# A decoder layer: folded cross-attention weights stored as two arrays, high and low, instead of one

## What is computed

```python
x = x + self_attention(layernorm(x), weight_qkv, weight_proj)   # 32 heads, 8 key/value groups, head size 128
x = x + cross_attention(layernorm(x), ctx, ctx, Wq, bq, Wk, bk, Wv, bv, interference, amp, Wo, bo)
x = x + ffn(layernorm(x), ...)                                  # low-rank weights multiplied out, one matmul

# in the cross attention, per projection:
y = z @ W.T + bias                       # reshaped to heads x 16 x 4
y = y + 0.1 * amp * einsum('bhsdi,hij->bhsdj', y, interference)
```

## Time and profile before

| | |
|---|---|
| median of three runs | 3618.52 us (3617.93 to 3620.3) |
| profiled execution, its own time | 3618.95 us |
| its span, first to last instruction | 3616.8 us |
| mean granted TensorE clock | 0.977 of full speed |
| busy in the span: PE / PE weight loads | 3440.5 us (95%) / 2677.0 us |
| busy: DVE / POOL / ACT | 1494.1 / 1250.3 / 1185.0 us |
| moved by DMA | 431.16 MB, mean 119 GB/s |
| self phase / cross phase / FFN (about) | 0 to 2036 / 2036 to 3268 / to 3617 us |

### The profile page before, as it was taken

The page is one execution under the profiler, slowest core; times in us unless marked ns, Lnnn a source line. Parts: engine busy times, 40 slices in busy tenths (PEclk is TensorE's granted clock), DMA queues, the critical chain, the costliest instruction groups (busy, mean ns, idle before and its releaser), DMA issues. The chain is left out here.

```text
span 3616.8 us, 49438 instructions
## 1 busy us (share of the span) xinstructions
PE 3440.5 (95%) x18100; PEld 2677.0 (74%) x18100; DVE 1494.1 (41%) x2238; ACT 1185.0 (33%) x1679; POOL 1250.3 (35%) x563
## 2 busy tenths in 40 slices
PE   6999999999999999999999679989979999998999
PEld 5888887888878888878787467767767777763587
DVE  3232332323332232423232446656656665652453
ACT  3232232323233232323222235445444454440110
POOL 4334343434324343434342334434334443320000
PEclk9999999999999999999999889999999999999999
DMA  4323233323333232332221254544555455534032
GB/s 168 106 94 113 89 135 130 115 93 106 127 128 117 93 110 93 128 134 89 85 93 53 108 150 128 173 146 137 156 152 137 129 161 162 141 88 157 35 133 76
DMA packets 137253, 431.16 MB, mean 119 GB/s; under 512 B 24112, under 2 KB 24112, under 8 KB 137144
## 3 DMA queue, kind: packets, MB, share of 16 engines
q1 hardware_dynamic: 131384, 408.58, 35.1%
q10 hardware_dynamic: 5760, 20.97, 1.4%
HBM read 316.21 MB, written 37.75 MB: 98 GB/s over the span
## 5 line engine op out<-in xcount | busy, mean ns | idle before, releaser
L446 POOL TENSOR_TENSOR sa_wl<-sa_wraw,sa_wh 128x1024 fp32r<-128x1024 f32 x192 | 458.2, 2402 | 777.3 <-ACT sa_wh L597 777.3
L53 PE MATMUL sa_u<-sa_ln_xh,sa_wh 128*128 128x512 f32 x1536 | 628.5, 409 | 4.4 <-DVE sa_ln_xl L254 4.4
L54 PE MATMUL sa_u<-sa_ln_xl,sa_wh 128*128 128x512 f32 x1536 | 599.7, 390 | 0.0
L55 PE MATMUL sa_u<-sa_ln_xh,sa_wl 128*128 128x512 f32 x1536 | 599.3, 390 | 0.0
L457 POOL TENSOR_TENSOR sa_pl<-sa_praw,sa_ph 128x1024 fp32r<-128x1024 f32 x128 | 318.0, 2516 | 446.4 <-ACT sa_ph L649 446.4
L53 PE MATMUL sa_pr<-sa_ph,sa_oh 128*128 128x512 f32 x1024 | 428.6, 419 | 0.1
L746 DVE TENSOR_TENSOR sa_acc<-sa_pr,sa_acc 128x512 f32<-128x512 f32 x256 | 176.9, 692 | 569.3 <-PE sa_pr L55 569.3
L54 PE MATMUL sa_pr<-sa_pl,sa_oh 128*128 128x512 f32 x1024 | 400.8, 391 | 0.0
L55 PE MATMUL sa_pr<-sa_ph,sa_ol 128*128 128x512 f32 x1024 | 400.0, 391 | 0.0
L738 DVE TENSOR_TENSOR sa_ol<-sa_o,sa_oh 128x512 fp32r<-128x512 f32 x128 | 88.6, 692 | 718.5 <-ACT sa_oh L661 718.5
L53 PEld LDWEIGHTS sa_u<-sa_ln_xh,sa_wh 128*128 128x128 f32 x1536 | 289.3, 188 | 83.6 <-issue 24.2
(11 more groups left out here) (185 smaller groups left out, 5765.7 us busy)
## 6 DMA issues: line engine op xcount, KB each, us to landing
sa_wraw<-in_wqkv SPq DMA_DIRECT2D x192, 512.0 KB, 3.5
sa_praw<-in_wproj SPq DMA_DIRECT2D x128, 512.0 KB, 3.5
ca_wraw<-w_folded SPq DMA_DIRECT2D x96, 512.0 KB, 3.2
ca_kstack<-ca_kmh SPq DMA_DIRECT2D x256, 128.0 KB, 2.4
ca_wraw<-in_wo SPq DMA_DIRECT2D x33, 512.0 KB, 4.2
ca_kstack<-ca_kml SPq DMA_DIRECT2D x128, 128.0 KB, 2.4
ca_qstack<-ca_qh SPq DMA_DIRECT2D x256, 64.0 KB, 2.5
sa_nat<-in_w_nat SPq DMA_DIRECT2D x24, 512.0 KB, 4.7
```

The lines of the kernel that those rows point to most:

```text
L53: nc.tensor.matmul(out, ah, bh, start=(first and i == 0), stop=False)
L54: nc.tensor.matmul(out, ah, bl, start=False, stop=False)
L55: ins = nc.tensor.matmul(out, al, bh, start=False, stop=(last and i == len(parts) - 1))
L446: nc.gpsimd.tensor_tensor(wl[:, u % 3], wraw[:, u % 3], f32(wh[:, u % 3]), ALU.subtract).then_inc(w_split, 1)
```

## The change

1. Self phase: ACT's copy of each fold half is now made to an fp32r tile `foldh`; DVE gets a new step `low_fold`, which subtracts it from the bank into `foldl`, and now DVE, not ACT, frees `v_ps` (`v_copied`). ACT waits for it before `store_fold`, which issues two stores of 512 KB instead of one.
2. Cross phase: SP loads high and low parts straight into `wh` and `wl` (two loads of 512 KB per chunk). ACT's copies and POOL's subtractions of key, query and value weights are gone. `wo` still comes raw and is split.
3. SP's order: a chunk's loads for the next step wait until PE has used the old one (`u_done`), no longer for a free raw buffer. The key's stand between the key stacks and the `wo` load, the query's behind the query stacks, the value's at the end of the step, ahead of a cross step's stores. The accumulator loads of the first step stand behind no weights of the next step.

```diff
@@ self_attention_phase: scalar
-            act.sem_inc(fold_stored, 16)
+            act.sem_inc(fold_stored, 32)
...
                     act.wait_ge(folded, m * 2 + (half + 3))
                     if half == 0:
-                        act.wait_ge(fold_stored, m * 16 + 16)
-                    nc.scalar.activation(fold[:, half * HALF:(half + 1) * HALF], v_ps[:], ACT.Copy
-                                         ).then_inc(v_copied, 1)
+                        act.wait_ge(fold_stored, m * 32 + 32)
+                    nc.scalar.activation(foldh[:, half * HALF:(half + 1) * HALF], v_ps[:], ACT.Copy
+                                         ).then_inc(fold_hi, 1)
...
                     act.wait_ge(v_copied, v0 + 4)
-                    act.dma_start(tile_of(w_folded, m), fold[:]).then_inc(fold_stored, 16)
+                    act.dma_start(tile_of(w_folded_hi, m), f32(foldh[:])).then_inc(fold_stored, 16)
+                    act.dma_start(tile_of(w_folded_lo, m), f32(foldl[:])).then_inc(fold_stored, 16)
@@ self_attention_phase: vector
+                def low_fold(half):
+                    if not s.steady:
+                        return
+                    dve.wait_ge(fold_hi, m * 2 + (half + 1))
+                    cols = slice(half * HALF, (half + 1) * HALF)
+                    nc.vector.tensor_tensor(foldl[:, cols], v_ps[:], f32(foldh[:, cols]), ALU.subtract
+                                            ).then_inc(v_copied, 1)
...
                 low_o(0)
                 next_moments(0)
+                low_fold(0)
                 low_o(1)
                 next_moments(1)
                 add_projected(0)
+                low_fold(1)
@@ cross_attention_phase: sync
-            def weights(n, item, g, skipped=0):
-
-                if not (isinstance(n, int) and n < 0):
-                    sp.wait_ge(w_split, splits(n, item + (-2), skipped))
...
+            def weights(u, g):
+                first = CH * WHICH[u]
+                sp.dma_start(f32(wh[:, u]), tile_of(w_folded_hi, g + first)).then_inc(w_loaded[u], 16)
+                sp.dma_start(f32(wl[:, u]), tile_of(w_folded_lo, g + first)).then_inc(w_loaded[u], 16)
+
+            def next_weights(s, u):
+                if s.nxt:
+                    sp.wait_ge(u_done, s.n * U + (u + 1))
+                    weights(u, s.next_g)
...
             def first_block():
-                weights(-1, KEY, 0)
+                weights(0, 0)
                 load_context(0, range(CRAW))
                 load(0, ln.x, ln.loaded)
-                weights(-1, QUERY, 0)
+                weights(1, 0)
                 load_context(0, range(CRAW, KC))
-                weights(0, OUT, 0)
-                weights(0, VALUE, 0)
+                weights(2, 0)
...
-                if s.nxt:
-                    weights(s.n, KEY, s.next_g)
-                    weights(s.n, QUERY, s.next_g)
...
-                    weights(s.n + 1, OUT, s.g, 0 if s.nxt else 2)
+                    next_weights(s, 0)
+                    sp.wait_ge(ow_split, s.n + 1)
+                    sp.dma_start(owraw[:], tile_of(wo, s.g)).then_inc(owraw_loaded, 16)
...
-                    if s.nxt:
-                        weights(s.n + 1, VALUE, s.next_g)
+                    next_weights(s, 1)
                 if s.norm:
                     load_context(s.b + 1, range(CRAW, KC))
+                if s.proj:
+                    next_weights(s, 2)
@@ cross_attention_phase: gpsimd
             def first_block():
-                weights(-1, KEY)
                 context_low(0)
-                weights(-1, QUERY)
             def step(s):
-                weights(s.n, OUT, 0 if s.proj else 2)
+                out_weights(s)
                 if s.proj:
-                    weights(s.n, VALUE)
                     mask_k(s)
-                if s.nxt:
-                    weights(s.n, KEY)
-                    weights(s.n, QUERY)
@@ cross_attention_phase: scalar
             def first_block():
-                weights(-1, KEY)
                 context_high(0, range(KC))
-                weights(-1, QUERY)
                 ln.deviations(act, 0)
...
                 copy_oT(0)
-                value_weights()
                 high_o(0)
                 high_unit(0, kh, km_ready, n * 2)
                 exps(1)
-                next_weights(KEY, 0)
                 copy_probs(1)
...
                 copy_probs(2)
-                next_weights(QUERY, 1)
```

More of the change, by code:

```diff
@@ L294, in pipeline, with self_attention_phase @@
     step(Step(b, 8, 0, proj=False, nxt=False, steady=False))
-def self_attention_phase(nc, sems, ident, causal_t, mix, eps, x_rows, wqkv, wproj, w_nat, w_folded, x1):
+def self_attention_phase(nc, sems, ident, causal_t, mix, eps, x_rows, wqkv, wproj, w_nat, w_folded_hi, w_folded_lo, x1):
     U = 2 + QPG
@@ L794, in cross_attention_phase @@
     STACK = 16 * PARTS * PAIRS
-    OUT, VALUE, KEY, QUERY = range(4)
-    ITEMS = 4
     DP = 32
@@ L852, in cross_attention_phase @@
         c_split = sem("ca_c_split")
-        wraw_loaded = [sem(f"ca_wraw_loaded{i}") for i in range(2)]
-        w_hi = sem("ca_w_hi")
-        w_split = sem("ca_w_split")
+        w_loaded = [sem(f"ca_w_loaded{u}") for u in range(U)]
+        owraw_loaded = sem("ca_owraw_loaded")
+        ow_hi = sem("ca_ow_hi")
+        ow_split = sem("ca_ow_split")
         u_done = sem("ca_u_done")
@@ L886, in cross_attention_phase @@
         block = ctx.enter_context(nc.Block())
-        high_weights = {OUT: owh[:], VALUE: wh[:, 2], KEY: wh[:, 0], QUERY: wh[:, 1]}
-        low_weights = {OUT: owl[:], VALUE: wl[:, 2], KEY: wl[:, 0], QUERY: wl[:, 1]}
-        def splits(n, item, skipped=0):
-            return n * ITEMS + (item + 3 - skipped)
         def pr_bank(t, half):
@@ L985, in _, with out_weights @@
             nc.gpsimd.memset(v[:, :, DK:DK + 1], 1.0).then_inc(v_set, 1)
-            def weights(n, item, skipped=0):
-                pool.wait_ge(w_hi, splits(n, item, skipped))
-                nc.gpsimd.tensor_tensor(low_weights[item], wraw[:, item % 2], f32(high_weights[item]), ALU.subtract
-                                        ).then_inc(w_split, 1)
+            def out_weights(s):
+                if not s.attn:
+                    return
+                pool.wait_ge(ow_hi, s.m + 1)
+                nc.gpsimd.tensor_tensor(owl[:], owraw[:], f32(owh[:]), ALU.subtract).then_inc(ow_split, 1)
             def context_low(b):
@@ L1040, in pieces @@
                         if k == 0:
-                            pe.wait_ge(w_split, [splits(n, KEY - ITEMS), splits(n, QUERY - ITEMS), splits(n, VALUE)][u])
+                            pe.wait_ge(w_loaded[u], n * 32 + 32)
                             if u == 1 and turns(s):
@@ L1136, in project @@
                     if t == 0 and half == 0:
-                        pe.wait_ge(w_split, splits(n, OUT, 0 if s.proj else 2))
+                        pe.wait_ge(ow_split, m + 2)
                     if half == 0:
@@ L1200, in _ @@
             act.sem_inc(probsT_ready, 1)
-            def weights(n, item, skipped=0):
-                act.wait_ge(wraw_loaded[item % 2], n * 32 + (16 * (item // 2) + 32 - 8 * skipped))
-                nc.scalar.activation(high_weights[item], wraw[:, item % 2], ACT.Copy).then_inc(w_hi, 1)
             def context_high(b, ks):
@@ L1240, in out_weights @@
                 def out_weights():
-                    if s.attn:
-                        act.wait_ge(pr_done, m * PR + 1)
-                    weights(n, OUT, 0 if s.proj else 2)
-                def value_weights():
-                    if s.proj:
-                        if s.attn:
-                            act.wait_ge(u_done, n * U)
-                        weights(n, VALUE)
-                def next_weights(item, u):
-                    if s.nxt:
-                        act.wait_ge(u_done, n * U + (u + 1))
-                        weights(n, item)
+                    if not s.attn:
+                        return
+                    act.wait_ge(pr_done, m * PR + 1)
+                    act.wait_ge(owraw_loaded, m * 16 + 16)
+                    nc.scalar.activation(owh[:], owraw[:], ACT.Copy).then_inc(ow_hi, 1)
                 def exps(t):
```

21 lines of the change are left out of this document (11 added, 10 removed).

## The result

The changed kernel takes 3633.99 us (median of 9 runs, 3622.76 to 3642.82), the kernel before 3620.27 us beside it (9 runs, 3616.75 to 3621.91): a ratio of 1.004, 95% interval 1.0031 to 1.0048. It is 0.4% slower, where 3611.0 us and a range of 3603 to 3624 were forecast. Rival A, slower, had been given 0.13. The profiled execution took 3636.05 us (span 3634.3), 17.1 us more than that of before.

The account below looks back on a forecast made before the run. PE was taken to bound the kernel, so only its 100 us of cross-phase gaps could be won. 3618.95 - 7.4 (first step) - 2.5 (third block change) + 2.0 (jumps) = 3611.05, predicted as 3611.0 us, range 3603 to 3624.

Parts of the forecast that it names:

- Rival A: Steady cross step: 1 MB queued in front lands the last query copy late, scores wait 31 times; 3626.5 us upward, chance 0.13.
- The steady step: Cross steps of 34.0 us: weight work already hidden, later loads still covered; cost 0, with thin cover.
- it should catch up: Steady step: query copies, some 3.7 us of queue in 8 us of issue, recover from 1 MB more in front; cost 0.
- The bound of 1 us per step: Steady step: upper limit on the loss, 0 to 1 us in each of 31 steps.
- rival C: Outer loop jumps: instruction fetch takes its turn among queues, waits stay 9.55 us; 3609.0 us in all, chance 0.15.
- First step: Start of cross phase: earlier mask and accumulators bring first scores from 2102.5 to 2095.1, a gain of 7.4 us.
- the bound of 0: First cross step: lower limit of its gain, if 1 MB of key weights burdens the queue as the accumulators did.
- the 1.0 taken out of 0 to 1.75: Start of cross phase: second half of context arrives later, partly offset by a saved copy; 1.0 us of loss.
- Block changes: Third cross step gains 2.5 us as ACT's weight wait goes; two loop jumps lose 1.0 us each, 2.0 in all.
- the gain of 2.5 us: After the third cross step: ACT no longer waits for weights, accumulators just in time; between 3.7 gain and 2 loss.
- The jumps: Two outer loop jumps: 1.5 MB more ahead of instruction fetches, 1.0 us loss each; sign: waits within 9 to 12 us.
- Self phase: 48 added DVE subtractions and 12.6 MB more stores stay hidden; cost 0, otherwise 1 to 2 us per norm step.

Follow-up runs that it names:

- new self phase: The kernel before with the changed self phase storing high and low arrays, cross phase as before on the high array: 3620.11 us, ratio 0.9999.
- dummies at the jump: The kernel before with four 0.5 MB dummy transfers on SP's queue in each block change, ahead of the stores: jump waits of 11.30 and 11.52 us.
- before, accumulators early: The kernel before with the first accumulators (2 MB) fetched ahead of the first step's next key and query weights: 3615.41 us, ratio 0.9986.
- output weights first: The changed kernel with output weights (0.5 MB) fetched before the key stacks, key weights left between key and query stacks: 3612.03 us, ratio 0.9985.
- both weights first: The changed kernel with key and output weights (1.5 MB) fetched before the key stacks: 3611.55 us, ratio 0.9979.
- fastest: The changed kernel with key and output weights before key stacks, value weights in their own step, block 0's query weights behind the context: 3600.61 us, ratio 0.9950.
- the other such pair: The fastest kernel with key and output weights put back between key and query stacks (3623.12 us), and the fastest itself (3600.61 us).

## Why the prediction was wrong

**The steady step (forecast 0, measured +16.1, and +4.0 in the first steps of blocks).** This is the step that failed, and rival A, at 0.13, had its mechanism and place. The sentence at fault is "it should catch up". It put 2.8 us on the 1 MB that joins, at 359 GB/s, and 3.7 us on the query copies. With the 0.5 MB already there that is 4.4 + 3.7 = 8.1 us for 2.36 MB from the last key copy's landing on, under the 11.0 us that are allowed. Measured were 12.2 us in the stalled step. The 359 GB/s came from a stretch with large transfers. Here small copies are mixed in with them, which the earlier trace rows had shown at 209 GB/s for the key stacks, and 2.36 MB at 209 GB/s are 11.3 us, over what is allowed. The slower rate stood in the prediction as a bound (4.8 us for the 1 MB, 5.0 with 1.05 MB), but it was put on one term only and the sum was never made against the 11.0 us.

What the sum left out besides are the loads issued behind the query copies, of which 0.7 MB were moved before the last copy had landed; how the 4.1 us of excess divide between the slower mix and these is not shown. The bound of 1 us per step was too low for its worst steps (2.4 us) and right for the mean, 0.8 us over the 24 steady steps. The two weighed causes were told apart: tiny transfers in that place leave steps of 34.0 us, bytes do not.

The Trainium skill, "DMA: Bandwidth & Descriptors", section on queues, rings and completion order, says that SP owns one ring on each of the same 16 DMA engines, and that each DMA engine consumes a ring's descriptors in ring order. The runs agree: the same 1.5 MB, ahead of the key stacks and not ahead of the query stacks, cost 22 us less. The same section's rule that an engine serves different queues in turn was rival C; the 2 MB ahead of the jump cost at most about 2 us, which fits it. By this second rule query copies on another engine's queue would take turns with the weights and not stand behind all of them. That wasn't tried.

**First step (forecast -7.4, measured -3.6).** Of the 3.6 us, 0.7 are an earlier start of the phase. PE's first matmul of the phase comes between 2044.65 and 2049.49 in the fourteen profiled executions, so times are counted from there:

| profiled execution | first matmul | first scores | from the one to the other |
|---|---|---|---|
| before | 2048.70 | 2102.47 | 53.8 |
| the same first step: new self phase; dummies at the jump | 2046.88; 2044.65 | 2099.88; 2095.58 | 53.0; 50.9 |
| before, accumulators early | 2048.67 | 2095.77 | 47.1 |
| changed | 2047.99 | 2098.90 | 50.9 |
| output weights first (key weights alone in the old place) | 2049.16 | 2096.52 | 47.4 |
| both weights first | 2047.67 | 2093.80 | 46.1 |
| fastest | 2048.96 | 2091.69 | 42.7 |

The mechanism was right: the accumulators moved early gain 3.8 to 6.7 us, by which execution of before they are set against. Two sizes were off. The weights in front of the query stacks cost something here as in a steady step: 4.8 us for the 1.5 MB, and 1.2 for the key weights alone, which is less than the 2.9 us by which single executions of the same first step differ. The text had the key weights as the bound of 0 and counted 0.8 us of issue. And the start lost 2.7 us (3.4 counted from the first matmul), not the 1.0 taken out of 0 to 1.75. Timeline of PE, its turn of the first normalised block, before and after:

```profile
2060.93 1.12 PE L237 MATMUL ca_x<-ident,ca_ln_x 128*128 128x128 f32 x4 [6.80 <-DVE ca_ln_x L229]
```
```profile
2063.59 1.12 PE L237 MATMUL ca_x<-ident,ca_ln_x 128*128 128x128 f32 x4 [10.14 <-DVE ca_ln_x L229]
```

The cause: the second half of the context let ACT begin 2.75 us later (2057.35 for 2054.60), as was worked out, but the saved copies gave nothing back, since nothing but the late context held that chain. The run with the query weights behind the context shows it: 12.0 us from PE's first matmul to this turn, 12.2 in before, 15.6 in the changed kernel.

**Block changes (forecast -2.5 and +2.0, measured +1.0 in all).** ACT's wait for weights went as said, and the accumulators became late as said (DVE waited 2.57 us, PE 2.01), so that the gain of 2.5 us was 1.6. The jumps stayed within 9 to 12 us. Missed was the norm step: SP sends the next block's activations right behind the 2 MB of query and value weights, and DVE waits for them (8.8 us in three steps, of which 4.7 reach the steps' length). The forecast had followed those 2 MB to the stores and the jump, and not to the load that stands directly behind them on the same queue.

**Self phase (forecast 0).** Right: 0.9999, and PE begins the cross phase's first matmul at 2047.99 where it was 2048.70, a difference that lies within the spread above.

**What the sum was worth.** With the one move that takes the key and output weights out of the way the kernel measures 3611.55 us, close to the forecast, but partly by luck, since errors cancel: its first step gains 8.7 where 7.4 were forecast (7.6 counted from the first matmul), and its norm steps lose 4.8 that weren't forecast. The profiled execution of before, too, stood at the slow end in the first step (a wait of 18.2 us, 13.8 in another execution of the same instructions).

## What to carry to other kernels

When loads are moved onto a shared queue ahead of copies that somebody waits for, sum all the bytes that must pass between two events at the slowest rate that the trace shows for any of them, and set the sum against the time from the one to the other; an issue that stays on time says nothing of the landing. Leave some slack, since the same bytes with the issues on time took 9.2 to 12.3 us here. Then follow the queue to the next load as well, and ask who waits for that. Where each load is put between the moment its buffer comes free and its first use is worth more here than the work that was saved: the same loads gave 3634 us in one order and 3601 in another.

## What the runs showed of the hardware

- 64 KB copies within the core behind 1.5 MB of weights: the DMA engines moved 248 GB/s in a stalled step, and the bytes up to the last query copy got through at an effective 194 GB/s, although a stretch of weights alone runs at about 400 (405 GB/s and a share of 1.03 from 2516.6 on, when the queue held nothing but weights).
- Two steps with the same issues at the same distances differ by 14% in the DMA engines' time per byte. On an edge like this one the time spreads: 3623 to 3643 us in the changed kernel and 3606 to 3618 with both weights first; 3613 to 3643 and 3601 to 3609 in the other such pair. The kernel before has 3611 to 3628 in 31 runs without such an edge, so that part of the spread is not of the queue.
- In the changed kernel a wait of PE of 2.20 us was followed by half the granted clock and a step 1.5 us longer, one of 2.14 us was not, nor were those of 0.3 and 1.3 us (granted clock 1.00 behind each). In the fastest kernel with the weights put back, those of 2.04, 2.10 and 2.37 us were. So waits of just over 2 us go either way here.
- The FFN phase, the same in all these kernels, takes 337 us in eight profiled executions and 340 us in six, with a granted clock of 0.96 and 0.95.

```profile
2516.60:2519.00 2.40, 2.40 (x15) 2.09 (x16) 1.66 (x2) 0.00 (x0) 0.00 (x0) 1.00 1.03 405
```
